# Second attention's first turns in a new order: last routed sums added early by GpSimd, rope ahead of picks, a bank of its own for the first q and k

## The reference, cut to what matters

```python
x = x + _L0_attn_ref(xn, ...) + _L0_ffn_ref(xn, ...)      # shared + routed sums end here
xn = _layernorm(x, axis=-1)
# _L1_attn_ref(xn): h is xn scaled by its rms and norm_w
q, k, v = (heads(Wq), heads(Wk), heads(Wv))
q, k = _apply_rope(q, cos, sin), _apply_rope(k, cos, sin)
M = M * f_t[..., None, None] + g_t[..., None, None] * scale * (k_t[..., :, None] * v_t[..., None, :])
y_t = jnp.einsum('bhd,bhde->bhe', q_t, M) * o_t[..., None]
# _L1_ffn_ref(xn): logits, top_k of them, gates, experts
logits = xf @ router_w + router_b
top_w, sel = jax.lax.top_k(logits, TOP_K)
```

## Time and profile before

| | us |
|---|---|
| median of 3 runs | 1636.55 (1634.8 to 1641.53) |
| the profiled execution | 1643.91 |
| its span, first to last instruction | 1642.2 |
| PE busy | 1543.8 (94%) |
| VectorE busy | 865.9 (53%) |
| ScalarE busy | 733.1 (45%) |
| GpSimd busy | 717.8 (44%) |
| mean granted clock of PE | 0.981 |

### The profile page before, as it was taken

One profiled execution on the slowest core, in us unless ns is written; L12 is line 12 of the kernel. 1 busy time (PEld: TensorE's weight loads), 2 busy tenths in 40 slices (PEclk: granted clock), 3 DMA queues, 4 the chain that ended last, 5 costly groups with the idle time before them and its releaser, 6 DMA issues.

```text
span 1642.2 us, 32345 instructions
## 1 busy us (share of the span) xinstructions
PE 1543.8 (94%) x10802; PEld 1184.8 (72%) x10802; DVE 865.9 (53%) x2424; ACT 733.1 (45%) x1923; POOL 717.8 (44%) x815
## 2 busy tenths in 40 slices
PE   6989989999989999999997799998999999999997
PEld 3545445555547999998665467767999899999996
DVE  6777897887822444442577778874222122222220
ACT  4544545565551323323656566644333343334332
POOL 3122235666532555553810467763333433333332
PEclk9999999999999999999998999999999999999999
DMA  8533325445305343444631385367333333333331
GB/s 271 128 113 93 89 79 99 93 103 99 87 4 237 106 114 111 114 115 120 207 103 65 103 222 104 79 102 293 58 54 53 51 57 53 55 59 58 53 55 23
DMA packets 154639, 167.60 MB, mean 102 GB/s; under 512 B 84820, under 2 KB 132816, under 8 KB 151408
## 3 DMA queue, kind: packets, MB, share of 16 engines
q1 hardware_dynamic: 129936, 128.15, 30.8%
q0 software_dynamic: 24544, 37.38, 10.5%
HBM read 104.10 MB, written 44.45 MB: 90 GB/s over the span
## 4 chain that ended last, share of the span: by engine, by line
PE 68%; DVE 9%; issue 8%; POOL 8%; DMA 3%; ACT 3%; SPq 1%; DVEq 0%; POOLq 0%; ACTq 0%
PE PS L1660 23%; PE PS L1678 22%; POOL SLOT L954 6%; PE PS L1517 4%; DVE PS L1980 3%; PE PS L1453 3%; PE PS L1502 3%; PE PS L1481 2%; PE PS L1463 2%; PE PS L1543 2%; PE PS L1634 2%; PE PS L1588 2%; POOL arena L1056 1%; POOL arena L1062 1%; ACT arena L1178 1%
## 5 line engine op out<-in xcount | busy, mean ns | idle before, releaser
L1660 PEld LDWEIGHTS PS<-arena 128*128 128x128 f32 x3408 | 398.3, 193 | 16.2 <-DVE arena L2201 4.9
L1660 PE MATMUL PS<-arena 128*128 128x128 f32 x3408 | 405.3, 276 | 3.5 <-DVE arena L2201 3.5
L1678 PE MATMUL PS<-arena 128*128 x1704 | 392.3, 379 | 0.0
L1678 PEld LDWEIGHTS PS<-arena 128*128 128x128 f32 x1704 | 312.4, 190 | 39.7 <-issue 0.2
L1980 DVE CUSTOM_DVE_ANT_0 PS<-PS,arena 128x512 f32<-128x512 f32 (+3 forms) x512 | 235.4, 523 | 46.0 <-PE PS L1481 41.9
L995 POOL DMA_INDIRECT out<-arena x71 | 111.6, 1573 | 296.4 <-ACT arena L1272 274.6
L1262 ACT ACTIVATE arena<-PS,arena 128x128 f32<-128x128 f32 x568 | 161.8, 368 | 138.3 <-PE PS L1660 135.9
L2226 DVE COPY arena<-arena 128x8 f32 x71 | 12.5, 175 | 348.3 <-ACT arena L1262 326.9
L928 POOL TENSOR_SCALAR_AFFINE_SELECT arena<-arena 128x256 f32<-128x256 f32 x256 | 99.5, 412 | 206.5 <-ACT arena L1178 206.1
L981 POOL DMA_INDIRECT arena<-XN,arena x142 | 145.8, 1027 | 100.4 <-PE PS L1645 40.6
L1178 ACT ACTIVATE arena<-PS 128x512 f32<-128x512 f32 (+1 forms) x256 | 166.3, 705 | 49.5 <-PE PS L1502 39.2
(11 more groups left out here) (248 smaller groups left out, 2031.4 us busy)
## 6 DMA issues: line engine op xcount, KB each, us to landing
arena<-FD SPq DMA_DIRECT2D x32, 512.0 KB
arena<-in_w SPq DMA_DIRECT2D x16, 1024.0 KB
SPL<-arena SPq DMA_DIRECT2D x32, 384.0 KB, 2.6
arena<-SPL SPq DMA_DIRECT2D x64, 192.0 KB
XN<-arena SPq DMA_DIRECT2D x16, 512.0 KB, 3.0
arena<-SPL SPq DMA_DIRECT2D x64, 128.0 KB
arena<-SUM SPq DMA_DIRECT2D x16, 512.0 KB, 6.8
arena<-in_x SPq DMA_DIRECT2D x8, 512.0 KB, 6.8
```

Of the source, the lines that this page charges most:

```text
L1660: ins = pe.matmul(o, m.now[i % 2][:, c * F + 128 * f:c * F + 128 * f + 128], m.xt[i % 2][:, 128 * c:128 * c + 128], start=(c == 0), stop=( ...
L1678: ins = pe.matmul(to, m.hT[i % len(m.hT)][:, 128 * c:128 * c + 128], m.WD[:, bass.ds(e * (nf * 256) + c * 256, 256)], start=(c == 0), stop ...
```

## The change

- `sum_load:7` goes from behind product 33 to behind product 22. `sums:7`, `combine:6` and `combine:7` go to behind product 28, and GpSimd does both combines. They no longer wait for `shared_add`; instead `shared_add` of batches 6 and 7 waits for them, and `stats` waits for `shared_add`.
- `stats:6` and `root:6` come earlier (products 33 and 34), `stats:7` and `root:7` stand behind product 39.
- The steps up to turn 0's end are written out as START. `rope:0` and `rope_add:0` come ahead of `picks:6`, `project_qk:1` ahead of `turn:0`, `project_qk:2` ahead of `affinity:0`. `decay:1` moves from behind product 39 to behind `rope_add:1`. The loop over TURN begins with n = 1 and leaves out what START has.
- `norm:7` is done by GpSimd, with a tensor_scalar of two factors for each of four tiles, ahead of `open:0`.
- The first q and k go into bank 1 (`qk_bank`), so that `project_qk:1` waits for no rope. The logits of batch 7 go into bank 1 as well, behind `rope:0`, instead of bank 7.
- `picks:7` goes from turn 1 to turn 2, `gates:1:4` from turn 5 to turn 7.

```diff
@@ -165,45 +165,38 @@
     19: "const1 sum_load:6 xt:2",
     20: "combine:4 picks:0",
     21: "root:3 stats:4 logits_copy:1 xa:2 root:4 scale:3 gates:0:0",
-    22: "shared_add:5:0 scale:4",
+    22: "shared_add:5:0 scale:4 sum_load:7",
     23: "logitsT:1 logitsT_copy:1 picks:1 norm:3",
     24: "logits:2",
     25: "sums:5 xt:3 shared_add:5:1 combine:5 logits_copy:2 logitsT:2 xa:3 logitsT_copy:2",
     26: "stats:5 norm:4",
     27: "logits:3",
-    28: "sums:6 logits_copy:3 logitsT:3",
+    28: "sums:6 combine:6 sums:7 combine:7 logits_copy:3 logitsT:3",
     29: "xt:4",
     30: "picks:2 logitsT_copy:3 root:5 gates:0:1 scale:5",
     31: "xa:4 gates:0:2 norm:5 picks:3",
     32: "gates:0:3 logits:4",
-    33: "sum_load:7 shared_add:6:0 shared_add:6:1 xt:5",
-    34: "logits_copy:4 xa:5 logitsT:4 combine:6 stats:6",
-    35: "logitsT_copy:4 picks:4 logits:5 logits_copy:5 root:6",
-    36: "decay:0",
-    37: "scale:6 logitsT:5",
-    38: "norm:6 sums:7 gates:0:4 xt:6",
-    39: "xa:6 decay:1 shared_add:7:0 logitsT_copy:5 picks:5 logits:6 logits_copy:6 logitsT:6 shared_add:7:1 logitsT_copy:6 picks:6",
+    33: "shared_add:6:0 shared_add:6:1 xt:5 stats:6",
+    34: "logits_copy:4 xa:5 logitsT:4 root:6",
+    35: "logitsT_copy:4 picks:4 logits:5 logits_copy:5 scale:6",
+    36: "norm:6 decay:0",
+    37: "logitsT:5",
+    38: "gates:0:4 xt:6 logitsT_copy:5",
+    39: "xa:6 shared_add:7:0 picks:5 logits:6 logits_copy:6 shared_add:7:1 stats:7 root:7",
 }
+START = ("project_qk:0 logitsT:6 project_val:0 rope:0 value:0 logitsT_copy:6 scale:7 rope_add:0 norm:7 open:0 project_qk:1 turn:0 "
+         "keys:0 turned:0 rope:1 project_val:1 value:1 rope_add:1 xt:7 decay:1 xa:7 open:1 project_qk:2 "
+         "affinity:0 logits:7 picks:6 weigh:0 decay_load:2 logits_copy:7 gates:1:0")
 TURN = [("state", -2), ("route", 0), ("project_val", 0), ("project_qk", 1), ("turn", 0),
         ("value", 0), ("turned", 0), ("decay", 0), ("update", -1), ("rope", 1), ("affinity", 0),
         ("sums_copy", -1), ("project_out", -1), ("keys", 0), ("weigh", 0), ("out_copy", -1), ("rope_add", 1),
         ("open", 1), ("decay_load", 2)]
 AMONG = {
-    (-1, "turn"): "combine:7 stats:7",
-    (-1, "keys"): "root:7",
-    (-1, "out_copy"): "scale:7 norm:7",
-    (0, "turn"): "xt:7",
-    (0, "turned"): "xa:7",
-    (0, "rope"): "logits:7",
-    (0, "keys"): "logits_copy:7",
-    (0, "weigh"): "gates:1:0",
-    (0, "out_copy"): "logitsT:7",
-    (0, "rope_add"): "logitsT_copy:7",
-    (1, "turn"): "picks:7",
-    (1, "update"): "gates:1:1",
+    (1, "affinity"): "logitsT:7 logitsT_copy:7 gates:1:1",
     (2, "decay"): "gates:1:2",
     (2, "sums_copy"): "gates:1:3",
-    (5, "rope_add"): "gates:1:4",
+    (2, "rope_add"): "picks:7",
+    (7, "rope_add"): "gates:1:4",
 }
 LATE = [s for s in TURN if s[0] not in ("weigh", "out_copy", "decay_load")] + [("weigh", 0), ("out_copy", -1), ("decay_load", 2)]
 
@@ -237,14 +230,15 @@
 
 
     route = iter([("route", p) for p in range(14, 20)] + [("scatter", i, (k,)) for i in range(NT) for k in range(2)])
-    out = []
-    for n in range(-1, NT):
+    out = list(steps(START))
+    begun = set(out)
+    for n in range(1, NT):
         for kind, ahead in TURN if n < NB else LATE:
             out += steps(AMONG.get((n, kind), ""))
             if kind == "route":
                 for _ in range(0 if n < 3 else 2 if n < 6 else 3 if n % 3 else 2):
                     out += [s for s in [next(route, None)] if s]
-            elif 0 <= n + ahead < NT and not (kind in ("decay", "decay_load") and n + ahead < 2):
+            elif 0 <= n + ahead < NT and (kind, n + ahead) not in begun and (kind, n + ahead) != ("decay", 0):
                 out.append((kind, n + ahead))
         if n % 8 == 1 and n > 8:
             out.append(("store_sums", n // 8 - 1))
@@ -565,7 +559,7 @@
         act_stat = sem("act_stat")
         root = sem("root")
         normed = sem("normed")
-        bank = {k: sem(f"bank{k}_read") for k in (4, 5, 6, 7)}
+        bank = {k: sem(f"bank{k}_read") for k in (1, 4, 5, 6, 7)}
         turned = sem("xn_turned")
         logit = sem("logit")
         logitT = sem("logitT")
@@ -643,15 +637,19 @@
 
         def on_pool(b):
 
-            return 0 < b < 6
+            return b > 0
+
+        def qk_bank(n):
+
+            return 1 if n == 0 else 0
 
         def logits_bank(b):
 
-            return 7 if b == NB - 1 else 6
+            return 1 if b == NB - 1 else 6
 
         def logits_read(b):
 
-            return (bank[7], f4[3] + 2) if b == NB - 1 else (bank[6], f4[2] + 2 * b + 2)
+            return (bank[1], 2) if b == NB - 1 else (bank[6], f4[2] + 2 * b + 2)
 
         def rooted0(b):
             return b + 1 if b < 2 else 4
@@ -1032,9 +1030,19 @@
 
             def combine(b):
                 pool.wait_ge(summed, b + 1)
-                pool.wait_ge(sh_added, 4 * b + 4)
+                if b < 6:
+                    pool.wait_ge(sh_added, 4 * b + 4)
                 pool.wait_ge(combined, b)
                 pool.tensor_tensor(ACC[:, 4 * b:4 * b + 4, :], ACC[:, 4 * b:4 * b + 4, :], G[2 * (b % 4)], ALU.add).then_inc(combined)
+
+            def norm1(b):
+                pool.wait_ge(normed, 16 + 2 * b + 2)
+                pool.wait_ge(xn_out[b % 2], 64 + 16 * (b // 2))
+                pool.wait_ge(turned, 16 + 2 * b - 2)
+                for j in range(4):
+                    i = 4 * b + j
+                    ins = pool.tensor_scalar(xn1[b % 2][:, j, :], ACC[:, i, :], RS[:, i:i + 1], NB1[:, i:i + 1], ALU.mult, ALU.add)
+                ins.then_inc(xn_made)
 
             def const1():
                 pool.memset(FT[:, :, 0:1], 0.0).then_inc(const1_set)
@@ -1088,6 +1096,8 @@
                     weights()
                 elif kind == "combine" and on_pool(a[0]):
                     combine(*a)
+                elif kind == "norm" and a[0] == NB - 1:
+                    norm1(*a)
                 elif kind == "const1":
                     const1()
                     bias_split()
@@ -1376,7 +1386,7 @@
                     b = a[0]
                     act.wait_ge(stat, 8 + 2 * b + 2)
                     act.activation(RS[:, 4 * b:4 * b + 4], MV[:, 4 * b:4 * b + 4, 1], ACT.Sqrt, bias=EPS[:, :]).then_inc(root)
-                elif kind == "norm":
+                elif kind == "norm" and a[0] < NB - 1:
                     norm1(*a)
                 elif kind == "xa":
                     b = a[0]
@@ -1722,7 +1732,7 @@
                 pe.wait_ge(bank[4], f4[0] + b + 1)
                 pe.wait_ge(nw_done, 2)
                 if b == NB - 1:
-                    pe.wait_ge(dk_mul, 4)
+                    pe.wait_ge(roped, 1)
                 elif b:
                     pe.wait_ge(bank[6], f4[2] + 2 * b)
                 bk = logits_bank(b)
@@ -1759,12 +1769,12 @@
 
             def project_qk(n):
                 i = ORDER1[n]
-                if n:
+                if n >= 2:
                     pe.wait_ge(roped, n)
-                else:
+                elif n == 0:
                     pe.wait_ge(nw_done, 4)
                 for c in range(2):
-                    ins = pe.matmul(ps(0, 0, 512), xnT[:, c, 128 * i:128 * i + 128], QKW[:, c, 0:512], start=(c == 0), stop=(c == 1))
+                    ins = pe.matmul(ps(qk_bank(n), 0, 512), xnT[:, c, 128 * i:128 * i + 128], QKW[:, c, 0:512], start=(c == 0), stop=(c == 1))
                 ins.then_inc(qk1)
 
             def project_val(n):
@@ -1828,7 +1838,7 @@
                     pe.wait_ge(yt_put, n)
                     pe.wait_ge(m_put, min(n, NST))
                 else:
-                    pe.wait_ge(bank[7], f4[3] + 2)
+                    pe.wait_ge(bank[7], f4[3])
                     pe.wait_ge(dk_mul, 4)
                 pe.wait_ge(vp_put, n + 1)
                 if n < NST:
@@ -1858,6 +1868,7 @@
                 if n:
                     pe.wait_ge(oe_put, n)
                 else:
+                    pe.wait_ge(bank[1], 2)
                     pe.wait_ge(const1_set, 12)
                 pe.matmul(ps(1, 256, 512), ident, ACC[:, ORDER1[n], :], start=True, stop=False)
                 pe.wait_ge(yt_put, n + 1)
@@ -2188,6 +2199,8 @@
             def shared_add(b, half):
                 i = 4 * b + 2 * half
                 dve.wait_ge(sh_down, i + 2)
+                if b >= 6:
+                    dve.wait_ge(combined, b + 1)
                 dve.tensor_tensor(ACC[:, i:i + 2, :], ps(2 + half, 0, 512).rearrange("p (i d) -> p i d", i=2), ACC[:, i:i + 2, :], ALU.add).then_inc(sh_added, 2)
 
             def tile_turn(layer, i):
@@ -2255,7 +2268,10 @@
                 dve.tensor_tensor(ACC[:, 4 * b:4 * b + 4, :], ACC[:, 4 * b:4 * b + 4, :], G[2 * (b % 4)], ALU.add).then_inc(combined)
 
             def stats1(b):
-                dve.wait_ge(combined, b + 1)
+                if b < 6:
+                    dve.wait_ge(combined, b + 1)
+                else:
+                    dve.wait_ge(sh_added, 4 * b + 4)
                 if b:
```

(2 more changed lines are left out.)

## The result

| | before | after |
|---|---|---|
| median, us | 1635.9 (20 runs, 1631.1 to 1641.68) | 1641.75 (20 runs, 1635.48 to 1646.81) |
| profiled execution, us | 1643.91 | 1641.93 |
| its span | 1642.2 | 1640.2 |
| PE / VectorE / ScalarE / GpSimd busy | 1543.8 / 865.9 / 733.1 / 717.8 | 1537.8 / 860.3 / 734.9 / 727.2 |

What follows compares the result with a forecast made beforehand. It took the stretch of waits on VectorE and GpSimd's open before turn 0 as the bound. Table loads +2.5, clock +2.7, order and norm:7 +0.4, combine -1.2, turn 7 +0.8: +5.2, to 1641.8; range 1633 to 1648.

Steps and rivals of the forecast that it cites:

- the walk to route 14: VectorE's path through turn 0 to the first operation of route part 14: 892.2 instead of 887.83, +4.4 us.
- The table loads: On ScalarE, root:6 ahead of the last gelu brings two loads of 1.28 us; that gelu ends at 849.6: +2.5.
- The rival of twice the load's cost: A function change on ScalarE costs twice its load: 2.56 us more at the gelu, 1644.3; chance 0.03.
- The clock behind the gap: PE idles 5.4 us before turn 0, then runs slower at the lower granted clock: +2.7 us.
- `norm:7` on GpSimd and the scan: norm:7 takes 2.9 us ahead of open:0, which decay:1's scan holds; turn 0 at 868.2; with the order, +0.4.
- The clean start: Rival: gelu is not held, PE keeps 2.4 GHz, open:0 gets ahead of the scan; 1635.1, chance 0.27.
- From there to route 14: VectorE from the end of affinity 0 to route part 14: 16.6 us, against 16.65 of work before.
- The early sums: Two combines leave VectorE for GpSimd; the second lay on the path: -1.21 us.
- Turn 7: gates:1:4 stands ahead of rope_add:8 on VectorE, open:8 follows: +0.8 us; a later decay_load:9 taken as 0, upper bound 3.
- The two unexplained waits: Waits in turns 7 (3.48 us) and 8, laid to no engine; may go with the moved weight loads, or grow.
- the rival in which the weight loads decide: The waits in turns 7 and 8 go, with a clean start, 1628.1; or two more come, 1648.8; chance 0.07.
- The falls at short gaps: Rival: PE's clock falls in gaps at 847.1 and before project_out:0, 2.67 and 2.3 us; 1646.7, chance 0.17.

Runs made afterwards that it cites:

- the version with all three undone: Changed kernel with root:6 behind the last gelu, norm:7 on ScalarE and gates:1:4 in turn 5: 1.0001 of the kernel before, 0.9953 when run again.

## Why the prediction came out right

The forecast was 1641.8, the median is 1641.75; the walk to route 14 gave +4.4, the profile shows +4.22. Point by point:

- *The table loads*: predicted +2.5, product start 849.6; measured +2.66 and 849.8, and undoing them gives 2.68 back. Right. The rival of twice the load's cost did not come: two loads and the small root between them made up the whole delay.
- *The clock behind the gap*: predicted 5.4 us of idling and 2.67; measured 5.60 and 1.8 (4.91 against 6.72 with PE kept busy). The place was right, the size 0.9 too high, which nearly cancels the 0.56 of turn 0 and the 0.16 of the loads: I took the row of 4.77 idling, and the other row, 1.6, was nearer.
- *`norm:7` on GpSimd and the scan*: predicted 2.9 for the norm (2.4 to 3.7), then `open:0` held by the scan to 868.15, and turn 0 at 868.2. Measured, on before's clock: the norm from 863.07 to 868.08, `open:0` behind it unheld, turn 0 at 868.76. The price was right: three of the four operations took 1.99 together, and with a fourth of 0.55 the norm would have been 2.5 (an estimate from its neighbours). The hold was right too, and its end, but it fell on the norm's last operation and not on `open:0`, whose own 0.6 came on top. That misplaced operation is about the 0.56 by which turn 0 is later than forecast. The norm's 5.01 is longer than the 5 on my list of signs of being wrong; what made it so was the scan that I had counted one operation later. The clean start failed on both its conditions: gelu was held, and nothing of `open:0` got ahead of the scan.
- *Affinity 0 ends*: predicted 875.5, measured 875.4. *From there to route 14*: predicted 16.6 to 16.7, measured 16.6. Right.
- *The early sums*: costed at -1.21; alone they gave -1.92 on VectorE at `stats:7` and -2.74 at route 14, with a clock that did not fall. I had seen the add of 1.61 beside `sums:7` and not priced what leaves with it. In the changed kernel `stats:7` follows `logits:6` and `shared_add:7:1`, with VectorE idle for 2.87 us before its copy of those logits, so the sum is not wrong by it.
- *Turn 7*: predicted +0.8, measured +0.9. The wait for `decay_load:9` is 2.13, within its bound of 3 us but not the 0 that I took, and I had no term for the later ones, the longest 4.83 at the scan of turn 12. The two unexplained waits went, as the rival in which the weight loads decide had it, but waits of the other shape took their place, and from turn 6 to 14 after gains only 0.7 on before.
- *The falls at short gaps* (chance 0.17) occur: at the first gap in four profiles of six, at the second in two of eleven, in both in one execution; measured 1.4 to 3.0 and some 1.5 and 1.7, predicted 2.67 and 2.3.

The median's +5.9 is more than the profile's end (+2.07) and a little more than the sum (+5.2). The match to 0.1 us is chance: the 1636.55 that I started from is 0.65 above the median of 20 runs, and the sum 0.65 below the measured difference; and route 14 of before alone moves by 3. The mean over the six profiles with the first gap is (0 + 0 + 3.0 + 1.4 + 1.6 + 1.65) / 6 = 1.3 us of lower clock, which after's own profile does not show; with route 14's 4.22 and turn 7's 0.9 that is 6.4. Before has such falls as well: with the mean of its two profiles, 64.4, in place of 62.88 it is 4.9. Four profiles that share after's steps up to route 14 have it at 67.07 to 68.61, two with before's at 62.88 and 65.90, so after is later there by 1.2 to 5.7. That this head makes the 5.9 of the medians is argued, not shown: the part behind route 14 moves by up to 8 us between executions. What stays open is what the waits laid to no engine wait for, and whether the version with all three undone really beats before: one batch says -0.5%, one says nothing.

## What to carry to other kernels

Place an operation that changes ScalarE's table where PE has work for the two loads, not ahead of the activation that feeds its next row. Moving work to an idle engine is worth nothing when it then stands in that engine's queue in front of what the path waits for: price it there, with what VectorE runs beside it, and read it operation by operation, since a row that sums four can hide one that was held. And read more than one profile before laying a microsecond at one stage to an edit, with the end of each counted from a common mark.

## What was new about the hardware

- PE's granted clock fell to 1.2 GHz behind an idle gap of 5.6 us in all five profiles that have it, behind 2.72 in four of six, behind 1.46 in two of eleven and behind 1.18 in one of three, in some executions and not in others of the same code; five unread products in the gap of 5.6 us kept it at 2.4 GHz.
- A GpSimd tensor_scalar of 128x256 took 0.54 us, and 3.05 when it began beside VectorE's `rope_add` and met the scan; a tensor_tensor of 128x256 took 0.61, and 2.53 beside a scan.
- A small VectorE add stood still for 1.4 us beside one GpSimd add of 1024 columns, and ran in 0.19 without it.
- The same program gave ratios of 1.0001 and 0.9953 in two batches, with intervals that do not meet.
